# The first bottleneck's 3x3 convolution by minimal filtering F(2,3); attention's transposes and 1x1 products a few steps earlier

## The reference, cut to what matters

```python
t  = silu(bn(conv1x1(gn(x), cv1_w)))                  # cv1, 512 -> 512
ys = [t[:, :256], t[:, 256:]]
for b in range(2):                                    # two blocks (bottlenecks)
    z = silu(bn(conv3x3(ys[-1], m_cv1_w[b])))         # 256 -> 256, padded by one
    q, k, v = split(conv1x1(z, m_qkv_w[b]))
    a = softmax(q^T (k + rw + rh) / 8)                # 4 heads, 1024 x 1024
    ys.append(ys[-1] + silu(bn(conv1x1(a v, m_cv2_w[b]))))   # "m2"
x = x + silu(bn(conv1x1(concat(ys), cv2_w)))          # cv2, 1024 -> 512
x = x + masked_conv1x1(gn(x))                         # layer 1, "l1"
```

## Time and profile before

| | before |
|---|---|
| median of three runs | 3309.7 us |
| the profiled execution: its time, its span | 3307.56 us, 3305.8 us |
| mean granted TensorE clock | 0.986 of full speed |
| PE busy | 3055.2 us, 92% |
| DVE, ACT, POOL busy | 55%, 49%, 35% |
| chain that ended last | PE 75%, DVE 8%, POOL 6%, ACT 5%, issue 4% |
| 3x3 matmuls (`y_pad,w_c`) | 3456 |
| conv of image 1 starts at | 602.03 us |

### The profile page before, as it was taken

One profiled execution on the slowest core, in us unless ns is written; L12 is line 12 of the kernel. 1 busy time (PEld: TensorE's weight loads), 2 busy tenths in 40 slices (PEclk: granted clock), 3 DMA queues, 4 the chain that ended last, 5 costly groups with the idle time before them and its releaser, 6 DMA issues.

```text
span 3305.8 us, 61456 instructions
## 1 busy us (share of the span) xinstructions
PE 3055.2 (92%) x27308; PEld 1564.0 (47%) x27308; DVE 1818.9 (55%) x2419; ACT 1617.1 (49%) x1922; POOL 1163.2 (35%) x864
## 2 busy tenths in 40 slices
PE   3679999999999999999999999999999999999997
PEld 3534544454544545445444545445454454445453
DVE  5636465465654555464654656546554646536463
ACT  1315475173833646255651838337462556518382
POOL 1114461063512462144611635124621446116151
PEclk8889999999999999999999999999999999999998
DMA  4200000100011000100001000110001000000001
GB/s 139 80 26 30 1 30 27 61 21 29 11 42 56 2 30 24 55 30 1 30 26 54 27 30 8 40 60 2 30 23 55 30 1 30 27 26 30 1 8 45
DMA packets 35896, 105.61 MB, mean 32 GB/s; under 512 B 12976, under 2 KB 15024, under 8 KB 32944
## 3 DMA queue, kind: packets, MB, share of 16 engines
q1 hardware_dynamic: 35632, 101.69, 8.6%
HBM read 80.18 MB, written 21.50 MB: 31 GB/s over the span
## 4 chain that ended last, share of the span: by engine, by line
PE 75%; DVE 8%; POOL 6%; ACT 5%; issue 4%; DMA 1%; SPq 0%; POOLq 0%; ACTq 0%; DVEq 0%
PE ps_u L686 44%; PE ps_u L848 13%; PE ps_o L870 4%; PE ps_o L871 3%; PE ps_u L822 3%; PE ps_o L872 3%; DVE row_max L1219 2%; PE ps_u L705 1%; ACT wide L1002 1%; POOL y_pad L1327 1%; POOL xn L1333 1%; ACT ps_u L1002 1%; POOL z L1327 1%; POOL wide L1327 1%; ACT qk L981 1%
## 5 line engine op out<-in xcount | busy, mean ns | idle before, releaser
L686 PE MATMUL ps_u<-y_pad,w_c 128*128 128x512 f16 x3456 | 785.3, 383 | 0.0
L1219 DVE TENSOR_REDUCE row_max<-ps_u 128x2 f32<-128x1024 f32 x512 | 616.5, 1221 | 230.2 <-PE ps_u L822 230.2
L1353 POOL TENSOR_TENSOR probs<-wide,probs 128x1024 f16<-128x1024 f32 x256 | 544.8, 2128 | 166.0 <-ACT probs L1006 154.6
L686 PEld LDWEIGHTS ps_u<-y_pad,w_c 128*128 128x128 f16 x3456 | 329.9, 97 | 420.7 <-issue 17.7
L1023 DVE SCALAR_TENSOR_TENSOR wide<-wide 128x512 f32<-128x512 f32 x256 | 183.4, 719 | 589.2 <-ACT wide L916 587.4
L848 PE MATMUL ps_u<-qk 64*128 64x512 f16 x3072 | 418.6, 378 | 65.6 <-ACT qk L981 26.4
L915 ACT ACTIVATE wide<-ps_u,par_m_t 128x512 f32<-128x512 f32 x128 | 99.3, 776 | 749.3 <-PE ps_u L686 749.3
L870 PEld LDWEIGHTS ps_o<-v_ext,probs 128*128 128x128 f16 x4096 | 375.6, 96 | 143.5 <-issue 122.2
L870 PE MATMUL ps_o<-v_ext,probs 128*128 128x65 f16 x4096 | 431.2, 193 | 0.0
L871 PE MATMUL ps_o<-v_ext,probs 128*128 128x64 f16 x4096 | 429.0, 195 | 0.0
L872 PE MATMUL ps_o<-v_ext,probs 128*128 128x65 f16 x4096 | 426.4, 191 | 0.0
(11 more groups left out here) (185 smaller groups left out, 4101.5 us busy)
## 6 DMA issues: line engine op xcount, KB each, us to landing
w_c<-w_c_dram SPq DMA_DIRECT2D x15, 2304.0 KB, 8.7
xn<-in_x_dram SPq DMA_DIRECT2D x32, 512.0 KB, 6.0
o_nat<-in_x_dram SPq DMA_DIRECT2D x64, 256.0 KB, 2.7
out_dram<-qk SPq DMA_DIRECT2D x32, 512.0 KB, 2.8
w_c_dram<-w_c SPq DMA_DIRECT2D x2, 2304.0 KB, 7.9
qk<-in_L_conv_m_cv_w_dram SPq DMA_DIRECT2D x2, 1152.0 KB, 7.2
probs<-in_L_conv_m_cv_w_dram SPq DMA_DIRECT2D x2, 1152.0 KB, 10.9
probs<-in_L_conv_cv_w_dram SPq DMA_DIRECT2D x2, 1024.0 KB, 12.7
```

The source lines that it names most:

```text
L686: ins = e.matmul(o, lhsT, rhs, start=start and k == 0, stop=stop and k == len(pairs) - 1)
L1219: e.reduce_max(row_max[:, g % 2, :, it, half], ps_u[:, use.slot:use.slot + 2, :], axis=AX.X).then_inc(*dve_max.up(i, b, g, half, it))
L1353: e.tensor_tensor(p_part(s, 1), wide[:, w.slot, :], p_part(s, 0), ALU.subtract).then_inc(*pool_lo.up("p", i, b, s))
```

## The change

**3x3 of block 0.** Two neighbouring outputs of a row come from four products in place of six. With d0..d3 the four inputs of a row and g0..g2 a row of weights: m0 = (d0-d2)g0, m1 = (d1+d2)(g0+g1+g2)/2, m2 = (d2-d1)(g0-g1+g2)/2, m3 = (d1-d3)g2 (signs as folded into the weights); outputs m0+m1+m2 and m1-m2-m3. The four kinds are the planes: `wino` holds them for the input, 12 units in `w_c3` for the weights (3 MB for block 0). A tile is 12 units x 2 input tiles x 3 terms = 72 matmuls of 256 columns into a pair of banks. Block 1 stays as it was.

**Planes.** New steps `sums` and `sums_lo`, four of each an image, one for each tile of cv1's second half: DVE makes the differences and sums in f32 (L1327 to L1329), ACT the edges and the hi parts, DVE the lo parts (L1335). For images 1 to 7 they stand among the layer-1 products; for image 0 directly behind each `cv1_lo`. cv1 runs m = 0, 1, 2, 3 in place of 2, 3, 0, 1.

**From banks to z.** In block 0 ACT copies plane 2 (x 0.5), DVE forms the two middle sums (2 x 256) and adds the outer planes interleaved (512), then tanh, scaled copy, silu; the hi part of z is now cast on ACT, in both blocks. The bank pair is free after DVE's interleaving add.

**Planning.** Block 0 has its own order, with three maxima ahead of the last tile's end where there were six; the group norm's steps move into block 0 and the early counts of block 1. Transposes start behind steps 20 and 21 (were 22 and 23), m2 behind 23 and 25 (were 25 and 27).

**The rest.** The two matmuls by `zeros` that opened each group of `av` (128 x 260 columns) go: the first product starts the bank. `o_nat` has half its size, so a group's normalise waits for that pair's former transposes, and `x_again` lies over all of it, so cv2's load of x waits for the last transposes where it waited for the first pair's. cv1's and block 1's maps lie in `y_rest`, unpadded; only block 0's output is padded. In setup POOL adds the taps for block 0's weights (three passes of 768 and a diagonal more for each of two groups), and 48 matmuls stand for 36.

```diff
-w_c3 = sb("w_c3", [P, 2, HT * TAPS, CH], F16)
+w_c3 = sb("w_c3", [P, 2, HT * UNITS, CH], F16)
...
-y_pad = sb("y_pad", [P, YT - HT, 2, HP * WP], F16)
+y_rest = sb("y_rest", [P, YT - 2 * HT, 2, HW], F16)
+y_pad = sb("y_pad", [P, HT, 2, HP * WP], F16)
+wino = sb("wino", [P, HT, 2, PLANES, HP * WT], F16)
...
-o_nat = sb("o_nat", [P, 2, JT, P], F32)
-x_again = o_nat[:, 0, :, :].rearrange("p a b -> p (a b)").rearrange("p (a n) -> p a n", a=2)
+o_nat = sb("o_nat", [P, 2, JT // 2, P], F32)
+x_again = o_nat[:, :, :, :].rearrange("p a b c -> p a (b c)")
...
+def wino_half(k, part, n):
+    return wino[:, k, part, :, (1 + n * ROWS) * WT:(1 + (n + 1) * ROWS) * WT].rearrange("p (h j) (r t) -> p h j r t", j=2, t=WT)
...
+def sums_view(w):
+    return sums_of(w).rearrange("p (h r t j) -> p h j r t", h=2, r=ROWS, j=2)
...
+def plane(use, q):
+    return ps_u[:, use.slot + q // 2, q % 2 * HALF // 2:(q % 2 + 1) * HALF // 2]
...
-for m in (2, 3, 0, 1):
+for m in range(CT):
...
+def plan_conv(i, b, m, n, row, k):
+    if (b, m, n) not in conv_use:
+        tile = (i, b, m, n)
+        freed_by = ("dve_u", ("m1_pairs", *tile)) if b == 0 else ("act_tile", ("m1", *tile))
+        conv_use[b, m, n] = banks.take(1.9, 50.0, freed_by, pair=b == 0)
+    plan("conv", i, b, m, n, conv_use[b, m, n], row, k)
...
+NORM_PARTS = {(1, 0, 0): 1, (1, 0, 1): 2, (1, 1, 0): 1}
+HALF_1 = (((("k", 1, 0), 0), (("v", 0), 2), (("v", 1), 2), (("k", 0, 1), 0), (("v", 2), 2), (("v", 3), 2), (("k", 1, 1), 0)),
+          ((("v", 0), 1), (("v", 1), 0), (("k", 0, 1), 0), (("v", 2), 2), (("v", 3), 2), (("k", 1, 1), 0)))
...
+if b == 0:
+    for m in range(HT):
+        plan_conv(i, b, m, 0, 2, 0)
+    for row in range(3):
+        plan_conv(i, b, 0, 1, row, 0)
+    next(ahead, None)
+    conv_end(0, 0)
+    conv_end(1, 0)
+    for row in range(2):
+        plan_conv(i, b, 0, 1, row, 1)
+    conv_end(0, 1)
+    for row in range(3):
+        plan_conv(i, b, 1, 1, row, 0)
+    next(ahead, None)
+    piece("q", 0, 0)
+    piece("k", 0, 0)
+    for row in range(2):
+        plan_conv(i, b, 1, 1, row, 1)
+        next(maxima)
+    piece("q", 1, 0)
     next(maxima)
+    conv_end(1, 1)
+    next(maxima)
...
-begins = {JT * 2 + 6: lambda: plan_transpose(i, b, 0, 0), JT * 2 + 7: lambda: plan_transpose(i, b, 1, 0),
-          JT * 3 + 1: lambda: threads.append(plan_m2(i, b, 0, 0)), JT * 3 + 3: lambda: threads.append(plan_m2(i, b, 1, 0))}
+begins = {JT * 2 + 4: lambda: plan_transpose(i, b, 0, 0), JT * 2 + 5: lambda: plan_transpose(i, b, 1, 0),
+          JT * 2 + 7: lambda: threads.append(plan_m2(i, b, 0, 0)), JT * 3 + 1: lambda: threads.append(plan_m2(i, b, 1, 0))}
...
+sums = planes_ahead(i + 1, new_maps) if i + 1 < B else iter(())
 for m in range(CT):
     for n in range(2):
         plan("l1", i, m, n, banks.take(2.6, 1.0, ("dve_x1", ("l1", i, m, n))))
+        if m < HT:
+            next(sums, None)
     plan("store", i, m)
+for _ in sums:
+    pass
...
+plan_sums(0, 0, step[2] - HT, step[3], step[5])
+plan_sums_lo(0, 0, step[2] - HT, step[3])
...
-def conv_rows(b, m, n, rows):
-    return [p for dy in rows for k in range(HT) for dx in range(3)
-            for p in three(lambda j: w_c3[:, j, k * TAPS + 3 * dy + dx, m * P:(m + 1) * P],
-                           lambda j: pad_view(b * HT + k, j, n * ROWS + dy, dx, ROWS))]
+def conv_rows(use, b, m, n, row, k):
+    w, (begin, end) = taps_of(b), ((row, k) == (0, 0), (row, k) == (2, HT - 1))
+    if b:
+        pairs = [p for dx in range(3) for p in three(lambda j: w[:, j, k * TAPS + 3 * row + dx, m * P:(m + 1) * P],
+                                                     lambda j: pad_view(k, j, n * ROWS + row, dx, ROWS))]
+        return products(ps_u[:, use.slot, :], pairs, start=begin, stop=end)
+    for q in range(PLANES):
+        terms = three(lambda j: w[:, j, k * UNITS + row * PLANES + q, m * P:(m + 1) * P],
+                      lambda j: wino[:, k, j, q, (n * ROWS + row) * WT:(n * ROWS + row + ROWS) * WT])
+        for at, (lhsT, rhs) in enumerate(terms):
+            ins = e.matmul(plane(use, q), lhsT, rhs, start=begin and q % 2 == 0 and at == 0, stop=end and q % 2 == 1 and at == 2)
+    return ins
...
+by_plane = (name, at[0]) == ("c3", 0)
+if by_plane:
+    cols, (dy, unit_at) = slice(q // UNITS * P, (q // UNITS + 1) * P), divmod(q % UNITS, PLANES)
+    w = src[:, m, cols, 3 * dy + 2 * unit_at] if unit_at < 2 else tap_sums[:, g % 2, unit_at - 2, cols, dy]
+else:
+    w = src[:, m, q // taps * P:(q // taps + 1) * P, q % taps]
...
-for bank in range(2):
-    e.matmul(ps_o[:, bank, 0:4 * (HD + 1)], ident16[:, :], zeros[:, :], start=True, stop=False)
...
-e.matmul(o, p_part(s, 0)[:, cols], v_ext[:, jt, h, 0:HD + 1], start=False, stop=False)
+first = jt == 0 and it % 2 == 0 and q == 0
+e.matmul(o, p_part(s, 0)[:, cols], v_ext[:, jt, h, 0:HD + 1], start=first, stop=False)
...
+def silu_halves_of(w, tile, name, t):
+    pt, py = par[name + "_t"], par[name + "_y"]
+    e.wait_ge(*dve_u.at("m1_pairs", *tile[1:]))
+    e.activation(wide[:, w.slot, 0:HALF], wide[:, w.slot, HALF:HW], ACT.Tanh, scale=pt[:, t, 0:1],
+                 bias=pt[:, t, 1:2]).then_inc(*act_copy.up("tanh", *tile[1:]))
+    e.wait_ge(*act_copy.now())
+    e.activation(wide[:, w.slot, HALF:HW], wide[:, w.slot, HALF:HW], ACT.Identity, scale=py[:, t, 0:1],
                  bias=py[:, t, 1:2]).then_inc(*act_tile.up(*tile))
...
-    silu_halves(("m1", i, b, m, n), use, w, "m1", b * HT + m)
+    if b == 0:
+        e.wait_ge(*u_full.at("m1", i, b, m, n))
+        until_free(e, w)
+        e.activation(wide[:, w.slot, 0:HALF // 2], plane(use, 2), ACT.Copy, scale=0.5).then_inc(*act_copy.up("m1_mid", i, b, m, n))
+        silu_halves_of(w, ("m1", i, b, m, n), "m1", b * HT + m)
+    else:
+        silu_halves(("m1", i, b, m, n), use, w, "m1", b * HT + m)
+    e.wait_ge(*dve_u.at("m1", i, b, m, n))
+    e.activation(z[:, m, 0, HH[n]], wide[:, w.slot, HALF:HW], ACT.Copy).then_inc(*act_cast.up("m1", i, b, m, n))
+elif kind == "sums":
+    i, b, k, n, w, w2 = a
+    e.wait_ge(*dve_u.at("sums", i, b, k, n))
+    if i:
+        e.wait_ge(*u_full.at("m1", i - 1, b, HT - 1, 1))
+    src, dst = sums_view(w2), wino_half(k, 0, n)
+    x, ends = img(wide[:, w.slot, HALF:HW]), img(sums_of(w2)[:, 0:HALF])
+    e.activation(dst[:, 1], src[:, 1], ACT.Copy)
+    e.activation(ends[:, :, 0:1], x[:, :, 1:2], ACT.Copy)
+    e.activation(ends[:, :, W - 1:W], x[:, :, W - 2:W - 1], ACT.Copy, scale=-1.0).then_inc(*act_copy.up("ends", i, b, k, n))
+    e.wait_ge(*act_copy.now())
+    e.activation(dst[:, 0], src[:, 0], ACT.Copy).then_inc(*act_cast.up("wino", i, b, k, n))
...
+elif kind == "sums":
+    i, b, k, n, w, w2 = a
+    x, ends = img(wide[:, w.slot, HALF:HW]), img(sums_of(w2)[:, 0:HALF])
+    mids, d = sums_view(w2)[:, 1], wide[:, w.slot, HALF:HW].rearrange("p (r t j) -> p j r t", r=ROWS, j=2)
+    e.wait_ge(*dve_u.at("cv1", i, HT + k, n))
+    until_free(e, w2)
+    e.tensor_tensor(ends[:, :, 1:W - 1], x[:, :, 2:W], x[:, :, 0:W - 2], ALU.subtract)
+    e.tensor_tensor(mids[:, 0], d[:, 0], d[:, 1], ALU.add)
+    e.tensor_tensor(mids[:, 1], d[:, 1], d[:, 0], ALU.subtract).then_inc(*dve_u.up("sums", i, b, k, n))
+elif kind == "sums_lo":
+    i, b, k, n, w2 = a
+    e.wait_ge(*act_cast.at("wino", i, b, k, n))
+    src, hi, lo = sums_view(w2), wino_half(k, 0, n), wino_half(k, 1, n)
+    for h in range(2):
+        ins = e.tensor_tensor(lo[:, h], src[:, h], hi[:, h], ALU.subtract)
+    ins.then_inc(*dve_lo.up("wino", i, b, k, n))
...
+if b == 0:
+    add, less = wide[:, w.slot, 0:HALF // 2], wide[:, w.slot, HALF // 2:HALF]
+    e.wait_ge(*act_copy.at("m1_mid", i, b, m, n))
+    e.scalar_tensor_tensor(less, plane(use, 3), -0.5, add, ALU.mult, ALU.add)
+    e.scalar_tensor_tensor(add, plane(use, 3), 0.5, add, ALU.mult, ALU.add).then_inc(*dve_u.up("m1_mids", i, b, m, n))
+    e.wait_ge(*dve_u.now())
+    e.tensor_tensor(wide[:, w.slot, HALF:HW].rearrange("p (n j) -> p j n", j=2), wide[:, w.slot, 0:HALF].rearrange("p (j n) -> p j n", j=2),
+                    ps_u[:, use.slot, :].rearrange("p (j n) -> p j n", j=2), ALU.add).then_inc(*dve_u.up("m1_pairs", i, b, m, n))
 silu_product(tile, w)
-e.wait_ge(*pool_hi.at(*tile))
+e.wait_ge(*act_cast.at(*tile))
...
+if n:
+    e.wait_ge(*a_full.at("o", i, b, pair, 0))
+elif b:
+    e.wait_ge(*a_full.at("o", i, b - 1, pair, 1))
...
+both_ends, less = tap_sums[:, g % 2, 0], tap_sums[:, g % 2, 1]
+small(e.tensor_tensor(both_ends, taps[:, :, :, 0], taps[:, :, :, 2], ALU.add), "tap_ends", g)
+small(e.tensor_tensor(less, both_ends, taps[:, :, :, 1], ALU.subtract), "tap_less", g)
+e.tensor_tensor(both_ends, both_ends, taps[:, :, :, 1], ALU.add).then_inc(*pool_small.up("tap_sums", g))
...
-elif kind == "conv_end":
-    i, b, m, n, use, w = a
-    e.wait_ge(*dve_u.at("m1", i, b, m, n))
-    e.tensor_scalar(z[:, m, 0, HH[n]], wide[:, w.slot, HALF:HW], 1.0, 0.0, ALU.mult, ALU.add).then_inc(*pool_hi.up("m1", i, b, m, n))
...
-e.wait_ge(*u_full.at("cv1", i - 1, 1, 1))
```

(3 more changed lines are left out.)

194 lines of the change are left out of this document (111 added, 83 removed).

## The result

| | before | after |
|---|---|---|
| median of 8 runs | 3309.4 us (3308.3 to 3310.7) | 3319.4 us (3314.9 to 3323.8) |
| ratio | | 1.003 (1.002 to 1.0039) |
| the profiled execution: its time, its span | 3307.56, 3305.8 us | 3323.83, 3322.1 us |
| PE busy | 3055.2 us | 2958.1 us |
| mean granted clock | 0.986 | 0.967 |

The account below looks back on a forecast made before the run. PE was taken to bound the kernel (busy 92%, 75% of the chain). Terms -66 + 13.6 - 14 - 9.8 + 8.8 - 14 + 11 = -70.4 gave 3237.2, as median 3239 us; range 3194 to 3282.

Parts of the forecast that it names:

- Block 0's matmuls: Block 0's 3x3 on PE: 288 matmuls at 0.110 us for 216 at 0.2203, 16.0 us less an image.
- The clock: PE's granted clock: low only behind image 0's wait for the planes, +1.6 us; 1.00 in block 0's windows.
- The chain and its waits: Block 0, banks to z: 5.8 us a tile, 9.9 us of PE waits for 2.6; net 8.3 an image gained, -66.
- Rival A: Block 0: ACT and DVE overlap tiles better, waits stay at 2.6; 58 us less, 3181 us; chance 0.12.
- rival B: Strided passes in block 0's chain and the planes cost double: +33, 3272 us; chance 0.17.
- rival D: Slower: PE's clock falls in each block 0 around the 3.3 us wait; 3327 us at 11 us an image; chance 0.05.
- Transposes and m2: Attention of both blocks: moved earlier, they remove PE's 1.2 us wait in each of 16 blocks; -14 (-19 to 0).
- x again: cv2's later load of x delays z's lo part and block 1's last m2 by 1.1 us an image; +8.8.
- Zeros: Product with v: 128 matmuls of 260 columns, 0.11 us each, leave PE's path; -14.
- cv2: cv2's operands: 96 of 192 matmuls an image read plain maps, 0.0127 us less each; -9.8.
- Setup: Setup: more PE matmuls, POOL's passes over the taps, the norms and a sixth bank set; +11 (5 to 15).
- Image 0: Image 0's conv waits for the planes, made behind cv1's tiles: +12, with the low clock +13.6 (5 to 16).

Follow-up runs that it names:

- e_fill: Changed kernel with useless 256-column matmuls (24, 18, 18) put into three waits of PE in each image: 3289.7 us.
- e_nochain: Changed kernel without the joining of the four planes in block 0 (ACT's copy and DVE's three passes left out, output not the reference's): 3259.1 us.
- e_hold: Changed kernel with the planner's hold of a finished conv tile's bank in block 1 back at 1.8 from 2.2: 3294.5 us.
- e_xa: Changed kernel with cv2's x loaded into the planes' inner rows, with the former wait for the first pair's transposes: 3299.1 us.

## Why the prediction was wrong, point by point

**Block 0's matmuls: right.** 288 of 256 columns in place of 216; the front without its dip is 62.2 us (e_fill), for 61.6 to 62.1. The clock of the forecast was the miss. By the figures of the Trainium skill, "TensorE: Matmul & The Clock Gate", section "Back-to-back issue gap", 256 columns would save nothing; in this trace the `wino` matmuls are 0.109 us apart, and those of 512 columns twice that.

**The chain and its waits: right,** 5.70 us, 1.74, 1.35, 0.84, 3.42. Rival A was worth 61 us (e_nochain), forecast as 58; rival B's strided passes cost nothing extra (256 elements at every second place took 0.42 us, the interleaving add 0.69).

**The clock: the step that failed.** The sum had no term for it behind image 0; it was rival D, at 0.05. I took the earlier trace rows (a wait of 2.66 us with the clock at 1.00) as proof that such waits are safe. The window there ends where the wait ends and doesn't show what follows; the trace has 1.00 behind it too, but that is one wait. The same wait, at the same place of image 1 and with the same 10.39 us of PE work in the 14.26 ahead of its end, stands in other traces. Windows behind it in before, in the changed kernel and in b_zeros (the kernel before without its zero matmuls):

```profile
680.31:684.50 4.19, 4.19 (x54) 2.18 (x54) 1.87 (x2) 3.08 (x3) 1.02 (x2) 1.00 0.00 0
...
699.11:703.00 3.89, 3.89 (x52) 1.98 (x52) 1.80 (x2) 2.78 (x3) 0.72 (x2) 1.00 0.00 0
...
679.87:684.00 4.13, 4.13 (x41) 2.15 (x42) 1.23 (x1) 3.02 (x3) 0.96 (x2) 0.64 0.01 4
```

It dips in the third, and in images 2 and 7 of the changed kernel. That the profile of before has no dip there was luck. Behind image 0's conv, 26 of the 31 waits of 2.4 us and more in the trace of after are followed by a dip, 2 of the 33 from 1.65 to 2.4, and none of the shorter ones. Nor does a busy stretch make a wait safe: in image 1 PE had been busy 11.53 of the 14.26 us ahead of the end of block 1's 2.73, more than the 10.39 of the wait that I called safe. What decides between two waits alike is open.

The profiled run missed the sum by 87 us (3323.8 for 3237.2): 47 are dips, 20 transposes and m2, 10 block 1's wait, 8 the zeros, 3 the setup, as the points below have them, and the rest nearly cancels. It is an estimate: what a dip costs PE isn't all seen at the end (e_fill). D's form was wrong as well: not one long slow stretch an image but 1.7 us behind each of three or four waits.

**Transposes and m2: the sign was wrong.** -14 was forecast, about +6 is in the profile: undisturbed attentions take 80.1 and 78.7 us for 80.0 and 78.7, though the zeros, 0.4 of each, had gone. The half with the transposes was right: with m2 at its old steps an attention gains 1.15 us, 0.4 of it the zeros', which leaves 12 us in all. The half with m2 I never priced: it put 1.4 us ahead of the normalise in DVE's full queue. "The skipped normalise waits end long before they matter" looked at the semaphore and not at the queue.

**Block 1's front: missing.** The prediction held block 1 unchanged. The banks are given out by a clock of estimates, a hold of 2.2 gave v's second product another bank, and the wait went from 1.44 to 2.73: 10 us, and its dips, 25 us together (e_hold).

**x again:** the last m2's wait is 2.47 to 2.70 for 1.35, 10 us in all where 8.8 were forecast; with its dips it is 21 us (e_xa). **Zeros:** 6 for 14. Perhaps these matmuls stand partly beside a wait; no run shows why. **cv2:** six matmuls take 1.29 us on `y_rest` and 1.38 on `y_pad`, 11 us in all, forecast 9.8. **Setup:** the first cv1 matmul at 207.96 for 193.72, +14.2 for 11. **Image 0:** conv starts 15.4 us later, setup's 14.2 among them, and waits 11.2 for the planes. The clock is then low for 10.2 us, but PE works in only 3.0 of them: 1.5 lost, as forecast (1.6).

POOL's three passes over the taps, second group, on its timeline:

```profile
101.67 1.50 POOL L1476 TENSOR_TENSOR w_cv<-probs 128x768 f32<-128x768 f32 x1
103.25 2.02 POOL L1477 TENSOR_TENSOR w_cv<-w_cv,probs 128x768 f32<-128x768 f32 x1
105.36 2.02 POOL L1478 TENSOR_TENSOR w_cv<-w_cv,probs 128x768 f32<-128x768 f32 x1
```

5.5 us, where 4.8 were forecast. The first pass, the fastest, reads two operands at a step of 12 bytes, the others one. By the Trainium skill, "GPSIMD Engine Reference", section "7. Performance pitfalls for Q7 kernels", 7.2 was worked out ahead; this trace does not bear it out.

## What to carry to other kernels

A change that takes work from the engine that bounds a kernel thins out its stretches; price each new wait twice, once for itself and once for the clock behind it, and don't take one wait at full clock as proof that its like is safe: look for it in every image and in other runs. When a step is moved, list what stands behind it in the queue of each engine it issues on; and where a planner hands out banks by estimates, compare its hand-outs before and after in the parts that were not changed. Useless matmuls in a known wait are a cheap test of whether the clock is what costs.

## What the runs showed of the hardware

- Dips of the granted clock to 1.2 GHz, mostly 3.4 us long, followed 64 of 71 waits of PE of 3 us and more, 133 of 196 from 2.4 to 3, 14 of 417 from 1.65 to 2.4, and none of 331 from 1.0 to 1.65 (all 17 traces, from behind image 0's conv to the last image's m2). The same wait in the same place dips in one run or image and not in another.
- DVE and POOL hold each other up: of a DVE pass of 0.69 us and a POOL pass of 1.12 that start within 11 ns, one takes 0.97 longer, and a difference of some 5 ns in the starts goes with which. A silu of DVE took 2.52 for 1.11 beside POOL's normalisation. The Trainium skill, "GPSIMD Engine Reference", section "1. Specifications", says that POOL's SBUF access contends with DVE instructions with two SBUF inputs; these rows agree.
- The kernel before has more than one speed: on one chip it took 3307 to 3311 us in eight runs and 3328 to 3336 in three, on another 3317 to 3331 in all eleven. Such ties may be behind it; that is not shown.
